# Flamingo block on one core: gathers, expert sums and K/Q/V projections of batches two to four moved between the items of the second attention, with a narrower causal mask

## The reference, cut to what matters

```python
x = x + tanh(g_xattn[0]) * L0_xattn(layernorm(x), ctx)
x = x + tanh(g_ffn[0])   * L0_ffn(layernorm(x))      # 16 experts, each token's best 4, and a shared one
x = x + tanh(g_xattn[1]) * L1_xattn(layernorm(x), ctx)
x = x + tanh(g_ffn[1])   * L1_ffn(layernorm(x))      # quantised product

# L1_xattn: 16 heads of 16 channels
q = x @ Wq;  k, v = split(concat(ctx, x) @ Wkv)      # 1024 queries, 64 + 1024 keys
dots = where(j > i + 64, -inf, q @ k.T * scale)      # causal, all context keys visible
out = softmax(dots) @ v @ Wout + bout
```

## Time and profile before

| what | us |
|---|---|
| median of 3 runs (1520.61 to 1525.6) | 1524.9 |
| the profiled execution, its own time | 1529.67 |
| its span in the profile | 1527.6 |
| PE, DVE, ACT, POOL busy, of the span | 1111.4, 1014.6, 637.1, 488.0 |

### The profile page before, as it was taken

How to read it: one execution, slowest core, us unless ns; L and a number is a source line. 1 busy time by engine, 2 the same in 40 slices (tenths; PEclk the granted TensorE clock), 3 DMA queues, 4 the chain that set the end, 5 groups by cost and what they waited for, 6 DMA issues and landing times. The chain is left out here.

```text
span 1527.6 us, 23799 instructions
## 1 busy us (share of the span) xinstructions
PE 1111.4 (73%) x8155; PEld 569.0 (37%) x8155; DVE 1014.6 (66%) x1856; ACT 637.1 (42%) x1280; POOL 488.0 (32%) x539
## 2 busy tenths in 40 slices
PE   4799984342409999705556469999999999998767
PEld 2455553121206666403232213333333333331546
DVE  4999975455545666445564488888888888870675
ACT  1455553111103333202122107777677777775430
POOL 1334331767760000077877141111111111111110
PEclk7999997666659999857676759999999999996889
DMA  6010100222279999833676421111211121100003
GB/s 207 21 35 29 42 1 18 87 86 86 92 263 224 246 265 249 223 108 91 209 230 193 135 80 39 38 39 46 56 51 38 39 61 53 39 2 1 1 0 110
DMA packets 183649, 146.24 MB, mean 96 GB/s; under 512 B 102638, under 2 KB 160494, under 8 KB 183546
## 3 DMA queue, kind: packets, MB, share of 16 engines
q1 hardware_dynamic: 162570, 102.61, 25.8%
q0 software_dynamic: 12288, 33.57, 6.8%
q10 hardware_dynamic: 8688, 8.66, 1.7%
HBM read 53.11 MB, written 68.55 MB: 80 GB/s over the span
## 5 line engine op out<-in xcount | busy, mean ns | idle before, releaser
L1783 DVE TENSOR_REDUCE small<-ps 128x2 f32<-128x960 f32 (+6 forms) x384 | 379.2, 1041 | 57.8 <-PE ps L1838 57.5
L1762 ACT ACTIVATE region<-ps 128x512 f32<-128x512 f32 (+5 forms) x768 | 343.2, 532 | 110.9 <-PE ps L1852 109.4
L1733 POOL TENSOR_SCALAR_AFFINE_SELECT region<-region 128x512 f32<-128x512 f32 (+2 forms) x160 | 87.3, 546 | 428.8 <-ACT region L1762 428.7
L1852 PE MATMUL ps<-region 50*128 50x512 f16 (+5 forms) x896 | 198.5, 332 | 26.7 <-ACT region L1762 23.5
L1928 PE MATMUL ps<-region 128*32 128x512 f32 (+5 forms) x1792 | 193.0, 504 | 2.5 <-POOL region L1733 1.9
L1201 PE MATMUL ps<-region 128*128 128x384 f16 x696 | 123.9, 329 | 39.5 <-DMA region<-expert_rows 39.1
L860 POOL DMA_INDIRECT expert_rows<-region,small x128 | 131.3, 1026 | 64.1 <-issue 35.9
L1838 PE MATMUL ps<-region 48*128 48x480 f16 (+6 forms) x896 | 141.7, 334 | 13.5 <-DVE small L1783 11.3
L1366 POOL DMA_INDIRECT region<-result_rows,home x128 | 135.0, 1055 | 38.0 <-issue 36.3
L1852 PEld LDWEIGHTS ps<-region 50*128 50x128 f16 (+1 forms) x896 | 54.3, 95 | 211.2 <-ACT region L1762 194.5
L1437 DVE SCALAR_TENSOR_TENSOR x_sb<-region,weights,x_sb 128x256 f32<-128x256 f32 x128 | 52.1, 479 | 70.5 <-DMA region<-result_rows,home 70.5
(11 more groups left out here) (237 smaller groups left out, 1693.1 us busy)
## 6 DMA issues: line engine op xcount, KB each, us to landing
result_rows<-region SPq DMA_DIRECT2D x58, 384.0 KB, 4.2
region<-v_parts SPq DMA_DIRECT2D x16, 576.0 KB, 3.9
v_parts<-region SPq DMA_DIRECT2D x14, 576.0 KB, 8.9
region<-k_parts SPq DMA_DIRECT2D x96, 68.0 KB, 2.2
region<-q_parts SPq DMA_DIRECT2D x96, 64.0 KB, 2.1
k_parts<-region SPq DMA_DIRECT2D x16, 272.0 KB, 5.0
x_sb<-in_x ACTq DMA_DIRECT2D x8, 512.0 KB, 9.4
region<-in_w13T SPq DMA_DIRECT2D x16, 256.0 KB, 3.0
```

Of the source, the lines that this page charges most:

```text
L1733: nc.gpsimd.affine_select(out=t, in_=t, compare_op=ALU.is_ge, fill=0.0, base=r0, pattern=[[0, G], [1, w]], channel_multiplier=-1).then_inc ...
L1762: nc.scalar.activation(dst, src, ACT.Exp, scale=SCALE).then_inc(s_exp, 1)
L1783: nc.vector.tensor_reduce(nmp[:, qt, :, p0:p0 + np_, place], s_pair(n + first)[:, :, 0:np_ * nk] .rearrange("p e (h k) -> p e h k", h=np_) ...
L1852: ins = nc.tensor.matmul(o, k_of(rr, tbuf)[:, pair, kt * P:kt * P + rows], q_of(rr, tbuf)[:, pair, q0:q0 + nq], start=True, stop=True)
```

## The change

Only chunks 0 and 1 (the first batch), and the gathers, sums and layer norm of chunk 2, stay in the projection stage. Half of chunk 3's gathers are issued there too. The rest is placed between the items of the attention units: in the prologue, and then in units 0 to 9. The new words are `G` (one gather), `C` (the sums of two tiles with one expert row), `B`, `A`, `W`, `R`, `M` (the layer norm's steps; `R` is POOL's), `X` and `x` (transposes, and the low part), `Q`, `K`, `V` (PE's products) with `q`, `k`, `v` (what frees their banks). `X`, `Q`, `K` and `V` each take a whole pair of `S_PAIRS` and hold it until the small letter. The table `BESIDE` says behind which `PV`, next `T` and next `S` of a unit each word stands. The bias is added in units 10 and 11 (`Y`). The second of the two mask products of a diagonal tile writes only the half of the columns in which it has anything. All engines' units are written out, with no hardware loop. SP stores batches 1, 2 and 3 in units 1, 4 and 9.

```diff
+        yg = view(region0, "yg", [P, 4, FETCH, TOPK, D], F32)
...
+        def store_parts(sp, b, ms, q_cols, k_cols, done):
+
+            for parts, dram, cols in ((qp, q_parts, q_cols), (kp, k_parts, k_cols)):
+                for part in range(PARTS):
+                    for a in range(2):
+                        sp.dma_start(dram[b, ms, a, part, :, cols].rearrange("k r n -> r k n"),
+                                     parts[64 * a:64 * a + 64, part, ms, cols]).then_inc(done, 16)
...
+        def buffer_of(c, t):
+
+            return (2 * (c % 2) + t, c // 2 + 1) if c < 4 else (2 + t, c - 1)
...
+                sp.wait_ge(s_dve, moved(turn[0, "k10"]))
+                store_parts(sp, 0, slice(0, KH), slice(0, CH), slice(0, CH), s_pfirst)
+                sp.wait_ge(s_dve, moved(turn[1, "k02"]))
+                store_parts(sp, 0, slice(0, 1), slice(CH, L), slice(CH, KEYS), s_pfirst)
+                sp.wait_ge(s_dve, moved(turn[1, "k12"]))
+                store_parts(sp, 0, slice(1, KH), slice(CH, L), slice(CH, KEYS), s_pstored)
+                sp.wait_ge(s_pfirst, FIRST_STORES)
+                load_parts(sp, 0, 0, s_unit0)
...
+                fetch(0, 0)
+                fetch(0, 1)
+                fetch(1, 0)
+                ln_pool(nc.gpsimd, 0, s_var, s_rstd)
+                fetch(1, 1)
+                nc.gpsimd.tensor_tensor(pause[:], half[:], half[:], ALU.pow).then_inc(s_pause, 1)
+                pool.wait_ge(s_pause, 1)
+                fetch(2, 0)
+                ln_pool(nc.gpsimd, 1, s_var, s_rstd)
+                fetch(2, 1)
+                fetch(3, 0)
+                ln_pool(nc.gpsimd, 2, s_var, s_rstd)
...
+                x_low(1)
+                low(1)
+                combine(2, 0)
+                combine(2, 1)
+                statistics(2)
+                normalised(2)
...
+        FIRST_ORDER = """G3.8 G3.9 G3.10 G3.11 G3.12 G3.13 G3.14 G3.15 X2.0 X2.1 S0 S1 x2.0 S2 S3 S4 S5
+                         Q2.0 S6 Q2.1 S7 S8 S9 q2.0 S10 S11 K2.0 S12 K2.1 S13 S14 S15 k2.0 S16 S17
+                         V2.0 S18 V2.1 S19 S20 S21 v2.0 S22 S23 mT0 N0 N1 N2 N3 N4 N5 N6 N7 N8 Tn0 Tn1"""
...
+            1: ("0 / Q3.0 / Q3.1 /", "1 / / G4.8 / q3.0", "2 / K3.0 / K3.1 / G4.9", "3 / / G4.10 / k3.0", "4 / K3.2 / G4.11 / C4.0",
+                "5 / / G4.12 / k3.2", "6 / V3.0 / V3.1 / G4.13", "7 / / G4.14 / v3.0 C4.1", "8 / V3.2 / G4.15 / C4.2",
...
+        def take(key, hold_):
+
+            free = [(slot + 1 + i) % FREE for i in range(FREE) if not held[(slot + 1 + i) % FREE]]
+            slot_of[key], before_of[key] = free[0], last_in[free[0]]
+            last_in[free[0]], held[free[0]] = key, hold_
+            return free[0]
...
+                def fetch(c, n):
+                    j, r = n // TOPK, n % TOPK
+                    if c > FIRST_C and n % (FETCH * TOPK) == 0:
+                        pool.wait_ge(s_comb, comb_at[c - 1, j // FETCH * TOPK + TOPK - 1])
+                    gather(nc.gpsimd, c, j, r)
...
-                            o = banks[half][:, 0:np_ * nk].rearrange("p (h k) -> p h k", h=np_)[:, :, nk - P:nk]
+                            o = banks[half][:, 0:np_ * nk].rearrange("p (h k) -> p h k", h=np_)
                             for part in range(2):
-                                nc.tensor.matmul(o, mask_id[rows[half], part, :], mask_dg[rows[half], part, 0:np_, :],
+                                nc.tensor.matmul(o[:, :, nk - P + part * HALF:nk], mask_id[rows[half], part, :],
+                                                 mask_dg[rows[half], part, 0:np_, part * HALF:P],
                                                  start=part == 0, stop=False, skip_group_check=True)
...
+                for u in range(UNITS - 1):
+                    if u + 2 < UNITS:
                         sp.wait_ge(s_pv, u * len(steps) + 2)
-                        load(u + 2, (r + 2) % NBUF)
+                        load(u + 2)
+                    if u == 9:
+                        store(3)
+                    maxima(u, (u + 1) % NBUF)
+                    if u in (1, 4):
+                        store({1: 1, 4: 2}[u])
```

789 lines of the change are left out of this document (469 added, 320 removed), and 26 rows, old and new, of the table BESIDE.

## The result

The changed kernel takes 1599.6 us, median of 4 runs (1592.65 to 1603.31), against 1524.9 (1520.61 to 1525.6): ratio 1.0514, 95% interval 1.0483 to 1.0545. It is slower by 5.1%, where 1463 had been forecast. The profiled execution took 1592.65 us, the fastest of its four; the one of the kernel before, 1529.67 us, was above all its timed ones. So the two profiles lie 63 us apart where the medians lie 75 apart.

What follows compares the result with a forecast made beforehand. Projection waits for POOL, the prologue for DVE, and a unit is a chain through PE, ACT and DVE. -140.6 + 14 + 65 + 4 - 4 = -61.6, so 1463 us from the median 1524.9; range 1430 to 1503.

Steps and rivals of the forecast that it cites:

- The projection stage, -140.6: Projection stage, waiting for POOL's gathers: with 56 gathers left in it, 731.2 in place of 871.8, -140.6 us.
- The mask and the loops, -4: Units: narrower mask products save 0.25 us over 16 units, 4 us; hardware loops written out give nothing.
- The prologue, +14 (4 to 24): Attention's prologue: gains chunk 2's low parts and PE pieces, partly hidden beside DVE's maxima; +14 us, 24 with nothing hidden.
- the turns on a single pair: Prologue: while a pair is held, PE and DVE take turns, 2 us a score instead of 1, for some six scores.
- Units 0 to 9, +65 (27 to 89): Units 0 to 9: inserted DVE and PE work, partly absorbed by idle time and waits, +65 us.
- nothing is absorbed: Units 0 to 9, upper end: each unit grows by the larger of its DVE and PE shares, 89 us.
- the larger of its two shares: Units 0 to 9: each unit grows by the larger of its inserted DVE and PE work; 65 us after partial absorption.
- A third of PE's pieces falls into waits for ACT: Units 0 to 9: pieces ahead of a T that would wait for ACT are one third absorbed; part of the +65.
- POOL, +4: Units: gathers, roots and bias additions delaying zeroings, together 4 to 15 us, taken as 4.
- the 0.7 us for each pair of sums, 28 us in all: Units: gathers lengthened by DVE's 40 pairs of sums through SBUF contention; would make the forecast 1487, not taken.
- The held pairs serialise, and the clock dips: Rival, units and prologue: nothing absorbed, one 1.6 us dip in each of nine units, 1511; chance 0.22 for 1483 to 1518.
- The clock stays low: Rival, units 0 to 8: clock at 0.50, 71 us a unit against 37.4; four such units make 1597; chance 0.05.

Runs made afterwards that it cites:

- the shared ring: Changed kernel with each piece in one bank of T's ring of three, one behind each PV, scores keeping both pairs: 1559.9 us, ratio 1.0291.
- Bare holds: Changed kernel with one matmul of six in each piece, and copies and low parts of 64 columns in place of 512: 1542.8 us.
- run 1600: Not a run's number: the changed kernel itself, with the whole change against the kernel before, measured 1599.6 us, ratio 1.0514.

## Why the prediction was wrong

**The projection stage, -140.6.** Nearly right: -133.9, and 129 to 134 by other traces. Counted from the stage's own start, which lies 4.3 us earlier than before's, DVE's normalising ended at 729.8 (725.5 + 4.3) where 730 was forecast. SP's queue is what ran over. Its last group of stores began at 720.8 on this count, not 717.5, and its 8 issues took 10.0 us, not 5 (1.25 us each, where the two groups ahead took 0.60 to 0.67). So the end is 737.9, behind even the 735 given for small issues that cost as much as large ones.

**The mask and the loops, -4.** Holds within its error: the mask alone measured -2 (-6 to +2).

**The prologue, +14 (4 to 24).** The mechanism stands, the size was too small: +24.1, the end for "nothing hidden". Without products the prologue took 38.3 us, as before the change, so the whole growth is theirs. The term that was mis-sized is the turns on a single pair, 6 us in my sum: with a pair of their own beside the scores' two the pieces cost 9.3 us less, and one bank at a time in the shared ring 19.0 less, for the same work. There the prologue grew by 5.0 us in all, so PE's pieces can be hidden beside DVE's maxima nearly whole, if they hold no pair of the scores.

**Units 0 to 9, +65 (27 to 89).** This is the step that failed: +174.9, outside even the end that was called "nothing is absorbed", and outside the 45 to 85 that were given as the mark of a wrong main step. Both ends took for each unit "the larger of its two shares". Two things are wrong in that.

First, the shares mostly add. Spreading the same pieces under the same sums gained nothing, where the larger of the two would have given some 20 us. Sums and layer norm alone cost 39.6, products without the sums 154.2 (465.9 - 311.7, layer norm included), and both together 174.9: at most 19 of 194 us are absorbed.

Second, and larger, a hold of a pair has a price of its own, which had no term; it was only a reason to choose a value nearer the upper end. By my list, units 1, 2, 4, 6 and 8, in which 23 of the 26 holds begin, were to grow by 6.5 + 7.1 + 8.0 + 7.1 + 8.0 = 36.7 us. Over 30.85 they grew by 26.1, 25.1, 33.2, 23.1 and 31.4, 139 in all. The other five were to grow by 28.3 and grew by 39. Bare holds alone measured 90.1 us. What that price is made of is shown in part only. Shortening the holds with all their work in them gave back 34.4 us, so the time for which a pair is held counts; the low clock behind PE's pauses is up to some 35. The rest lies between turns on the single pair and the round trip of each piece through three engines that take their work in order. The second need not be small: in the ring, with both pairs left to the scores, the units were only 13.8 us shorter. ACT's copies had no term either, since I listed DVE's and PE's shares only: copies and low parts measured 25.8.

"A third of PE's pieces falls into waits for ACT" also fails. PE's weight loads did wait 40 us less for ACT than before (76.5 against 116.3), but ACT stood 115 us longer for PE's `T` (180.6 against 65.4). My reading is that a piece put ahead of a `T` that would have waited makes the next exponential late.

**POOL, +4.** PE's weight loads stood 17.0 us for POOL's zeroing in units 0 to 9, against 6.4 before. In the run without sums and gathers it was 8.5, so the term was some 10 us and not 4, about half of it from sums and gathers. But no gather grew long: the 64 in the units took 0.94 to 1.13 us each, median 0.95, although 80 sums ran on DVE there. So the 0.7 us for each pair of sums, 28 us in all, did not come. The 1.67 us of the earlier trace rows was no rule before either: 15 of the 128 gathers took over 1.2 us, and two inside DVE's next eight sums took 1.02 and 1.26. The rival was put beside the Trainium skill, "GPSIMD Engine Reference", section "Key points"; the units show no contention of that size. What cost most at a time is a root that stands ahead of a zeroing and waits for DVE. In unit 5 the zeroing at 1088.80 stood behind one, and `PV` waited 3.98 us for it, where perhaps 2 had been allowed:

```profile
1087.77 1.04 POOL L234 TENSOR_TENSOR rstd<-ve,half 128x4 f32<-128x4 f32 x1 [4.64 <-DVE ve L1981]
```
```profile
1089.48 1.72 PE L2104 MATMUL ps<-region 128*32 128x448 f32 x8 [3.98 <-POOL region L1820]
```

In the run without any sum or gather unit 5 still grew by 7.2 us (38.1 against 30.85, its clock at 0.87), and unit 7, whose root comes late in it, by 0.8.

**The rivals.** "The held pairs serialise, and the clock dips" was the right mechanism and far too small: 85 + 14 us for the units, against 174.9. Its sign, PE's weight loads behind the maxima for more than 6 us a unit, came in (7.2), and so did the clock under 0.9. I had one dip of 1.6 us in each of nine units; the trace has two to four stretches at the low level in each unit with several holds (two in unit 4 with six holds, four in unit 8 with five). The sign for DVE did not come: it was busy 0.60 to 0.79 of units 0 to 3, not 0.9. "The clock stays low" gave 1597 and the run 1600, but not for its reason: no unit stayed at 1.2 GHz, and with a sixth of the products unit 4 had a clock lower by 0.18 than the changed kernel's and was 2.1 us shorter. That its 1597 met the measured time is chance. The Trainium skill, "TensorE: Matmul & The Clock Gate", section "A second HAM failure mode: psum-queue depth-cycling", describes frequent short idle times of PE while it cycles through PSUM banks, and a clock that goes up and down with them; it doesn't say how many banks. These units agree: PE's weight loads stand for up to 1.8 us for a maximum, and the clock goes from 1.00 to 0.52 and back in the slices above.

What stays open: the clock's part of a hold, between nothing and 35 us; how the rest divides between the single pair and the round trip; and whether a ring that really keeps `T` off a piece's bank would beat the kernel before.
